# A graph network's degree counts moved into the building stage, and the edge-maximum passes' buffers moved into adjacency tiles

## The chip, the cores and the metric

The kernel runs on one core of a Trainium2 chip as one launch. The metric is the device time of that core in microseconds. It is given as the median of several runs, and one more execution was recorded by the profiler. "Before" and "after" are two versions of one kernel on the same inputs.

## The reference, cut to what matters

The network has 3125 nodes with 96 features and 50000 edges from `src` to `dst`, sorted by `dst`. There are four residual stages, each behind a layer norm and a ReLU. Stage 0 is an attention over the edges with four heads. Stage 1 is two pooling layers, the part that the change touches most. Stage 2 is a sum over weighted edges, stage 3 sixteen steps of propagation.

```python
def _sage_pool_layer(x, src, dst, Wp, bp, Ws, Wn, b, n_nodes):
    m = jax.nn.relu(x @ Wp + bp)
    msgs = m[src]
    agg = jax.ops.segment_max(msgs, dst, num_segments=n_nodes)
    agg = jnp.where(jnp.isfinite(agg), agg, 0.0)
    return x @ Ws + agg @ Wn + b
...
edge_index = jnp.stack([src, dst])
h = jnp.maximum(_layernorm(x, axis=-1), 0.0)
x = x + _L0_gnn_ref(h, L0_gnn_qW, L0_gnn_kW, L0_gnn_vW, src, dst)
h = jnp.maximum(_layernorm(x, axis=-1), 0.0)
x = x + _L1_gnn_ref(h, src, dst, L1_gnn_Wp1, L1_gnn_bp1, L1_gnn_Ws1, L1_gnn_Wn1, L1_gnn_b1, L1_gnn_Wp2, L1_gnn_bp2, L1_gnn_Ws2, L1_gnn_Wn2, L1_gnn_b2)
h = jnp.maximum(_layernorm(x, axis=-1), 0.0)
x = x + _L2_gnn_ref(h, src, dst, edge_weight, L2_gnn_weight_G, L2_gnn_bias_G)
h = jnp.maximum(_layernorm(x, axis=-1), 0.0)
x = x + _L3_gnn_ref(h, edge_index)
```

## The kernel before, in words

**Stages.** Nodes are padded to T = 25 tiles of P = 128 (NP = 3200). The program is a row of stages, each with a block of instructions per engine, and a stage begins when all engines have ended the one before: `front`, `build_adjacency`, `walk_adjacency` (its body is a branch for inputs that overflow the building windows, not taken here), `attention`, `first_layer` (the first dense stage), `max_pass` "max1", `second_layer`, `max_pass` "max2", `third_layer`, `sum_pass` (a branch too), `weighted_layer`, `propagate`. Engines meet through semaphores alone. The order on each engine is the order in which its block writes the instructions.

**`build_adjacency`** makes `adj`, a 3200 x 3200 matrix of fp16 edge counts, 25 tiles `adj[:, k, :]` of 128 partitions by 3200. It works in NGROUP = 200 groups of GROUP = 16 destination nodes. For each group VectorE builds one-hot matrices (ScalarE the first lane matrix, L1260), TensorE multiplies three pairs of them into PSUM (`count`, L1250), and ScalarE copies the result to `adj` (L1269). TensorE's product of a group waits for `kept` of two groups earlier. GpSimd splits the edge weights into two fp16 parts at the start of the stage, SyncE then stores the tables and loads v and the first queries.

**`attention`** works through `adj`, and SyncE saves the last AWAY = 3 tiles of `adj` to DRAM (`away_dram`), since the maximum passes use that place: for the pooled features as two fp16 parts (`pooled_parts`) and, behind them, for one-hot matrices and ids.

**`first_layer`** loads the attention's result, adds it, normalises, and multiplies by the joint weights, tile by tile. On TensorE `turn` (L215) transposes a tile and `multiply` applies the weights. Beside them, `count(n)` (L227) multiplies the columns of one adjacency tile by a column of ones, 25 matmuls a call, to add up every node's degree; eight calls stand ahead of the first tile, one behind each of the first seventeen tiles. ScalarE's first `keep_high`, which writes over the saved tiles, waits until their three are counted. VectorE copies the degrees to `c.deg` at the end of the stage.

**`max_pass`** takes the running maximum over the sorted edges, in NB = 98 blocks of BLK = 512 edges, and beside it builds the weight matrix that `weighted_layer` needs. The blocks m go round one loop, which is written out on each engine; block n = m - 4 is scanned while group m of the weight matrix is laid out. For a block:
- GpSimd gathers 4 x 128 rows of the table in DRAM by index (`indirect_dma_start`, L1736), four gathers a block, into one of RING = 4 row buffers. It waits for `turned`. The eleven blocks in `FAR` are not gathered: TensorE multiplies the pooled parts by one-hot matrices (`add_far`, L1766).
- TensorE transposes the rows (`turn_rows`, L1757), lays out the weight strip (`lay_out`, L1776), spreads the mask (`spread_same`), turns pieces of the finished weight tile (`turn_piece`, L1786) and turns the scanned block back (`turn_back`, L1797).
- VectorE scans (`scan`, L1852: run = max(same x run, column)), builds the next one-hot matrices (L1831, L1833) and keeps the strip's low part.
- ScalarE keeps the mask, the strip's high part (L1919), the turned pieces in `rows_w` (`keep_piece`, L1926) and the turned rows in `out` (`keep_rows`).
- SyncE stores `out` to `rows_dram` (L1968) and, once every four blocks, a finished weight tile from `rows_w` to `weights_dram` (`store_tile`, L1955), two DMAs of 400 KB.

There are two `out` buffers and one `rows_w` buffer. ScalarE's first copy of a piece into `rows_w` for tile i waits for both stores of tile i - 1:

```python
if q == 0 and i >= 1:
    act.wait_ge(rows_stored, 32 * i)
```

TensorE's `turn_piece` waits for ScalarE's copy of the piece before, and `turn_back` stands behind it on TensorE. At the end of a pass (m >= 100) there are no new blocks to lay out, and two pieces are turned at each m. In the first pass alone, TensorE multiplies `upper` (a triangle of ones, made by GpSimd in `first_layer`) and `c.ones` by the degrees, and VectorE's `find_ends` (L1867 on) works out from it the row of every node's last edge, `c.end_row`, which the following dense stages gather by.

In the second pass SyncE loads the three saved tiles back once the last `FAR` block is summed. **`third_layer`** gathers by `c.end_row`, and ends with a copy between halves of the last adjacency tile on SyncE, for which the stage waits.

## Time and profile before

| | us |
|---|---|
| median of 3 runs | 2963.13 |
| lowest and highest | 2960.17, 2963.28 |
| the profiled execution | 2987.34 |
| its span | 2985.5 |
| TensorE busy in the span | 2539.4 (85%) |
| VectorE | 1983.1 (66%) |
| ScalarE | 1225.4 (41%) |
| GpSimd | 1213.3 (41%) |

The mean granted TensorE clock of the profiled execution was 0.914 of full speed. The span is the time from the first to the last recorded instruction. The profiled execution took 24 us more than the median of the runs without a profile, so a sum made from its rows is set against its own time first.

The profile's page calls the engines PE (TensorE; PEld is its weight load, which overlaps the matmuls), DVE (VectorE), ACT (ScalarE), POOL (GpSimd) and SP (SyncE); SPq, POOLq and PEq are their queues. A row names the line of the kernel, the engine, the operation and the tiles, out<-in. A bracket at its end gives the engine's idle time before it and what ended it; "issue" is a wait for nothing that the profile shows, "remote" one for a semaphore without a named setter. The stages lie in the span at about: `front` 0 to 61, `build_adjacency` to 270, `attention` to 678, `first_layer` to 731, the first maximum pass to 1295, `second_layer` to 1376, the second pass to 1934, the third dense stage to 2026, `weighted_layer` to 2170, `propagate` to the end.

### The profile page before, as it was taken

How to read it: one execution, taken by the hardware profiler on the slowest of the kernel's cores; microseconds unless marked ns; L12 is line 12 of the kernel's file. 1: busy time of each engine (PE TensorE's matmuls, PEld its weight loads, DVE VectorE, ACT ScalarE, POOL GpSimd, SP SyncE). 2: the span in 40 equal slices, each digit the busy share in tenths (PEclk: the TensorE clock that was granted, in tenths of full speed). 3: DMA queues.
4: the chain of work that ended last, by engine and by line, in shares of the span. 5: the costliest groups of instructions: out<-in, count | busy, mean ns of one | idle time of the engine just before them, and what ended most of it. 6: DMA issues, size and time to landing. Idle time of an engine off the chain costs nothing. (4 is left out here: it accounts for less than half of the span.)

```text
span 2985.5 us, 67875 instructions
## 1 busy us (share of the span) xinstructions
PE 2539.4 (85%) x26431; PEld 1862.9 (62%) x26431; DVE 1983.1 (66%) x6098; ACT 1225.4 (41%) x2932; POOL 1213.3 (41%) x1428
## 2 busy tenths in 40 slices
PE   6998999997778877747788887557899999999999
PEld 3223777775444444424444444336689999999999
DVE  6998999995788887726889888541234444444444
ACT  5998888884334343423334443330121111111110
POOL 2002999992677776633777777421000000000000
PEclk8999999996999888856999999758999999999999
DMA  6002000004344344442444444517800000000000
GB/s 194 1 1 69 12 12 13 12 11 110 93 110 120 102 105 109 104 85 56 114 102 120 107 105 110 146 44 268 282 5 2 2 2 2 2 2 2 2 2 18
DMA packets 239010, 205.59 MB, mean 69 GB/s; under 512 B 183165, under 2 KB 204442, under 8 KB 238144
## 3 DMA queue, kind: packets, MB, share of 16 engines
q1 hardware_dynamic: 210892, 162.00, 19.5%
q0 software_dynamic: 24256, 37.90, 5.2%
q8 instruction: 214, 3.51, 0.5%
q10 hardware_dynamic: 3540, 1.30, 0.2%
q14 instruction: 108, 0.88, 0.1%
HBM read 103.06 MB, written 100.41 MB: 68 GB/s over the span
## 5 line engine op out<-in xcount | busy, mean ns | idle before, releaser
L1736 POOL DMA_INDIRECT max_row<-table,max_src_rows x696 | 768.6, 1104 | 399.2 <-issue 246.5
L2329 PE MATMUL prop<-g,adj 128*128 128x192 f16 x9216 | 770.6, 246 | 7.1 <-PEq L2000 7.1
L2329 PEld LDWEIGHTS prop<-g,adj 128*128 128x128 f16 x9216 | 759.5, 98 | 14.9 <-issue 12.4
L1630 POOL TENSOR_SCALAR e<-e 128x512 f32<-128x512 f32 (+1 forms) x625 | 365.8, 604 | 244.6 <-ACT e L1618 226.9
L1644 DVE TENSOR_TENSOR e<-e,a_ps 128x1024 f32<-128x1024 f32 (+1 forms) x313 | 371.6, 1194 | 35.1 <-PE a_ps L1556 13.8
L2418 ACT ACTIVATE g<-prop_state 128x96 f16<-128x96 f32 (+1 forms) x375 | 106.0, 283 | 635.1 <-DVE prop_state L2386 635.1
L1618 ACT ACTIVATE e<-s_ps 128x512 f32<-128x512 f32 (+1 forms) x625 | 335.5, 585 | 61.0 <-PE o_ps L1568 38.1
L1776 PE MATMUL max_strip_ps<-max_key_hot,max_lane_w 128*128 128x400 f16 x1200 | 311.4, 369 | 57.3 <-DVE max_lane_w L1833 30.3
L2384 DVE SCALAR_TENSOR_TENSOR part<-prop,coef,prop_base 128x96 f32<-128x96 f32 x384 | 120.5, 314 | 312.8 <-PE prop L2329 226.1
L1926 ACT ACTIVATE max_rows_w<-max_piece 128x896 f16<-128x896 f16 x200 | 168.0, 840 | 378.7 <-remote 164.6
L1833 DVE TENSOR_SCALAR max_lane_w<-iota,max_tables 128x128 f16<-128x128 f16 x1200 | 320.6, 314 | 0.0
L1852 DVE TENSOR_TENSOR_SCAN max_run<-max_same,max_run,max_col 96x512 f32<-96x512 f16 x174 | 221.1, 1271 | 142.6 <-issue 116.0
L1766 PE MATMUL max_far<-adj 128*96 128x512 f16 x1100 | 277.1, 391 | 4.1 <-issue 3.2
L1776 PEld LDWEIGHTS max_strip_ps<-max_key_hot,max_lane_w 128*128 128x128 f16 x1200 | 101.4, 104 | 205.8 <-issue 122.8
L1831 DVE TENSOR_SCALAR max_key_hot<-iota,max_tables 128x400 f16<-128x400 f16 x600 | 188.1, 313 | 35.6 <-remote 17.0
L1250 PE MATMUL count<-key_hot,lane_hot 128*128 128x400 f16 x600 | 195.0, 342 | 19.2 <-ACT lane_hot L1260 7.4
L1766 PEld LDWEIGHTS max_far<-adj 128*96 128x96 f16 x1100 | 139.9, 128 | 109.8 <-issue 17.9
L1568 PE MATMUL o_ps<-e,v_all 128*25 128x128 f32 (+1 forms) x5000 | 197.6, 276 | 5.0 <-DVE e L1644 2.7
L1919 ACT ACTIVATE max_strip<-max_strip_ps 128x400 f16<-128x400 f32 x200 | 101.1, 506 | 244.5 <-PE max_strip_ps L1776 165.9
L1786 PE MATMUL max_piece<-ident,max_strip 128*128 128x128 f16 x1250 | 110.4, 229 | 102.0 <-ACT max_rows_w L1926 76.1
L1546 PE MATMUL s_ps<-q_tile,k_all 96*128 96x128 f16 (+1 forms) x2500 | 190.6, 219 | 4.6 <-DMA k_all<-qk_dram 4.6
L1786 PEld LDWEIGHTS max_piece<-ident,max_strip 128*128 128x128 f16 x1250 | 88.9, 103 | 161.4 <-issue 137.1
(260 smaller groups left out, 3334.2 us busy)
## 6 DMA issues: line engine op xcount, KB each, us to landing
weights<-max_rows_w SPq DMA_DIRECT2D x100, 400.0 KB
rows_dram<-max_out SPq DMA_DIRECT2D x196, 192.0 KB
ws_w<-weights SPq DMA_DIRECT2D x50, 384.0 KB, 5.2
ws_w<-weights SPq DMA_DIRECT2D x50, 288.0 KB, 4.5
max_row<-table,max_src_rows POOLq DMA_INDIRECT x696
ws_w<-weights SPq DMA_DIRECT2D x50, 128.0 KB, 2.7
adj<-ids_dram SPq DMA_DIRECT2D x22, 128.0 KB
q_tile<-qk_dram SPq DMA_DIRECT2D x100, 24.0 KB
```

The source lines that it names most:

```text
L1250: mm = nc.tensor.matmul(count_ps[g % 2][:, 0:KEYS], lane_hot[:, g % RINGS, w, :], key_hot[:, g % RINGS, w, :], start=w == 0, stop=w == WIN ...
L1568: mm = nc.tensor.matmul(o_ps[row % 2][hd * VW:hd * VW + DH + 1, 0:w], v_all[:, t, hd, :], e_tile(u)[:, hd * w:(hd + 1) * w], start=t == 0, ...
L1618: nc.scalar.activation(e_tile(u), s_ps[u % S_RINGS][:, 0:HEADS * width(row)], ACT.Exp).then_inc(exped, 1)
L1630: nc.gpsimd.tensor_scalar(e_tile(u), e_tile(u), math.exp(10.0), math.exp(-10.0), ALU.min, ALU.max).then_inc(clipped, 1)
L1644: nc.vector.tensor_tensor(tile, tile, a.unsqueeze(2).to_broadcast([P, n, HEADS, w]), ALU.mult).then_inc(weighted, 1)
L1736: nc.gpsimd.indirect_dma_start(row[i % RING][:, j, :], None, table_dram, bass.IndirectOffsetOnAxis(ap=src_rows[:, 4 * n + j:4 * n + j + 1] ...
L1766: mm = nc.tensor.matmul(far_ps[0:D, :], parts[:, k, a, :], hot[(T * j + k) % HOTS], start=k == a == 0, stop=k == T - 1 and a == 1)
L1776: mm = nc.tensor.matmul(strip_ps[n % 2][:, 0:KEYS], lane_w[:, w, h, :], key_hot[:, w, :], start=w == 0 and h == 0, stop=w == WIN - 1 and h ...
L1786: tr = nc.tensor.transpose(piece_ps[:, k * P:(k + 1) * P], strip[:, i % 2, first_tile[q] + k, :, :].rearrange("p h d -> p (h d)"), c.ident ...
L1833: one_hot = nc.vector.tensor_scalar(lane_w[:, w, h, :], c.iota16[:, 0:P], at(1), at(2 + h), ALU.is_equal, ALU.mult)
L1852: nc.vector.tensor_tensor_scan(run[n % 2][:, :], same[n % SAME][:, :], cols[0:D, :], run[1 - n % 2][:, BLK - 1:BLK], ALU.mult, ALU.max).th ...
L2329: return nc.tensor.matmul(sums(step, t), adj[:, k, t * P:(t + 1) * P], states[:, k, :], start=start and t % 2 == 0, stop=k == END - 1 and ...
```

## The change

- **Building.** USED_GROUPS = 196 groups are built instead of 200; GpSimd clears the columns of the last four in all tiles. The 625 one-column matmuls that add up the degrees are placed on TensorE between the groups' products, about three ahead of each group, for node tiles whose groups are finished; the last 25 follow the last group. VectorE copies the degrees to `c.deg` at the end of the stage. The branch of `walk_adjacency` counts again, behind its own additions.
- **`first_layer`.** The counting goes out, and with it ScalarE's wait. The two matmuls by `upper` and by `c.ones` and `find_ends` come in, TensorE's ahead of the first transpose, VectorE's ahead of the first group's sums. They go out of the first maximum pass.
- **Five tiles saved.** AWAY is 5 and NEAR_END 3: `attention` saves the last five adjacency tiles. The last three serve as before (`pooled_place`). The two before them (`buffer_place`) hold, in the maximum passes, a second `rows_w` and the third and fourth `out`. The second pass loads the last three back, `third_layer` the two others, behind its copy between the halves, and waits for them at its end.
- **`max_pass`.** `keep_piece` waits for the tile before the previous one, with a semaphore for each buffer; `keep_rows` for the block four earlier. `turn_back` takes every fourth column of the scanned block, so that a partition holds four consecutive rows, and the store to `rows_dram` writes them as one piece.

The diff, cut to its core:

```diff
@@ -48,6 +48,8 @@
...
+USED_GROUPS = -(-N // GROUP)
...
@@ -63,7 +65,8 @@
...
-AWAY = 3
+AWAY, NEAR_END = 5, 3
...
@@ -220,18 +224,9 @@
...
-            def count(n):
...
-                for t in range(T):
-                    mm = nc.tensor.matmul(deg_ps[:, t:t + 1], adj[:, k, t * P:(t + 1) * P], c.ones16[:, :], start=n == t == 0, stop=n == T - 1, skip_group_check=True)
-                if n == AWAY - 1:
-                    mm.then_inc(place_counted, 1)
-                if n == T - 1:
-                    mm.then_inc(counted, 1)
-            for n in range(EARLY):
-                count(n)
+            pe.wait_ge(upper_made, 1)
+            nc.tensor.matmul(ends_ps[:, 0:T], upper[:, :], c.deg[:, :], start=True, stop=True)
+            nc.tensor.matmul(ends_ps[:, T:2 * T], c.ones[:, :], c.deg[:, :], start=True, stop=True).then_inc(ends_summed, 1)
...
@@ -272,9 +265,6 @@
...
-                if g == 0:
-                    act.wait_ge(place_counted, 1)
...
@@ -342,7 +332,25 @@
...
+            def find_ends():
...
+                dve.wait_ge(ends_summed, 1)
...
+                then_wait(nc.vector.tensor_copy(total[:, :], ends_ps[:, T:2 * T]), 1)
+                then_wait(nc.vector.tensor_tensor_scan(before[:, :], c.ones[:, 0:T], total[:, :], 0.0, ALU.mult, ALU.add), 2)
...
+                nc.vector.tensor_copy(c.end_row[:, :], cum[:, :])
...
+            find_ends()
...
@@ -614,7 +620,10 @@
...
+            sp.dma_start(buffer_place(adj), away_dram[:, 0:(AWAY - NEAR_END) * NP]).then_inc(away_loaded, 16)
...
+            sp.wait_ge(away_loaded, 16)
...
@@ -1237,18 +1247,37 @@
...
+            dve.wait_ge(degrees_counted, 1)
+            nc.vector.tensor_copy(c.deg[:, :], deg_ps[:, 0:T])
...
-            for g in range(NGROUP):
+            def count(t, k):
+                return nc.tensor.matmul(deg_ps[:, t:t + 1], adj[:, k, t * P:(t + 1) * P], c.ones16[:, :],
+                                        start=t == k == 0, stop=k == T - 1, skip_group_check=True)
+            for g in range(USED_GROUPS):
...
+                t, i = divmod(g - 1 - TILE_GROUPS, TILE_GROUPS)
+                if t >= 0:
+                    for k in range(T * i // TILE_GROUPS, T * (i + 1) // TILE_GROUPS):
+                        count(t, k)
...
+            t, i = divmod(USED_GROUPS - 1 - TILE_GROUPS, TILE_GROUPS)
+            for k in range(T * i // TILE_GROUPS, T):
+                count(t, k)
+            pe.wait_ge(kept, USED_GROUPS)
+            pe.wait_ge(rest_cleared, 1)
+            for k in range(T):
+                mm = count(T - 1, k)
+            mm.then_inc(degrees_counted, 1)
...
@@ -1447,15 +1479,30 @@
...
-def away(adj):
-    return adj[:, T - AWAY:T, :].rearrange("p k n -> p (k n)")
+                pe.wait_ge(added, STEPS)
...
+                mm.then_inc(recounted, 1)
+def away(adj, first, last):
+    return adj[:, first:last, :].rearrange("p k n -> p (k n)")
+def pooled_place(adj):
+    return away(adj, T - NEAR_END, T)
+def buffer_place(adj):
+    return away(adj, T - AWAY, T - NEAR_END)
...
-    return away(adj)[:, 0:T * 2 * D].rearrange("p (t a d) -> p t a d", t=T, a=2)
+    return pooled_place(adj)[:, 0:T * 2 * D].rearrange("p (t a d) -> p t a d", t=T, a=2)
@@ -1517,7 +1564,7 @@
...
-            sp.dma_start(away_dram, away(adj)).then_inc(away_stored, 16)
+            sp.dma_start(away_dram, away(adj, T - AWAY, T)).then_inc(away_stored, 16)
...
@@ -1674,12 +1720,15 @@
...
-        out = [sb(f"out{i}", [P, 4, D], F32) for i in range(2)]
+        more = buffer_place(adj)
+        out = [sb(f"out{i}", [P, 4, D], F32) for i in range(2)] + [
+            more[:, T * P + 8 * D * i:T * P + 8 * D * (i + 1)].bitcast(F32).rearrange("p (j d) -> p j d", j=4) for i in range(2)]
...
-        written = [sem(f"written{i}") for i in range(2)]
+        written = [sem(f"written{i}") for i in range(OUTS)]
+        rows_stored = [sem(f"rows_stored{i}") for i in range(2)]
...
@@ -1687,18 +1736,15 @@
...
-        rows_w = sb("rows_w", [P, T, P], F16)
+        rows_w = [sb("rows_w", [P, T, P], F16), more[:, 0:T * P].rearrange("p (k n) -> p k n", k=T)]
...
@@ -1791,15 +1837,11 @@
...
-                elif upper is not None:
-                    pe.wait_ge(sums_read, 2)
...
-                    tr = nc.tensor.transpose(back_ps[:, j * D:(j + 1) * D], run[n % 2][:, j * P:(j + 1) * P], c.ident[0:D, 0:D])
+                    tr = nc.tensor.transpose(back_ps[:, j * D:(j + 1) * D], run[n % 2][:, j:BLK:4], c.ident[0:D, 0:D])
...
-            if upper is not None:
-                nc.tensor.matmul(back_ps[:, 0:T], upper[:, :], c.deg[:, :], start=True, stop=True).then_inc(ends_summed, 1)
-                nc.tensor.matmul(back_ps[:, T:2 * T], c.ones[:, :], c.deg[:, :], start=True, stop=True).then_inc(ends_summed, 1)
...
@@ -1920,17 +1939,17 @@
...
-                if q == 0 and i >= 1:
-                    act.wait_ge(rows_stored, 32 * i)
-                nc.scalar.activation(rows_w[:, first_tile[q]:first_tile[q] + PIECES[q], :].rearrange("d k p -> d (k p)"),
+                if q == 0 and i >= 2:
+                    act.wait_ge(rows_stored[i % 2], 32 * (i // 2))
+                nc.scalar.activation(rows_w[i % 2][:, first_tile[q]:first_tile[q] + PIECES[q], :].rearrange("d k p -> d (k p)"),
...
-                if n >= 2:
-                    act.wait_ge(written[n % 2], 16 * (n // 2))
-                nc.scalar.activation(out[n % 2][:, :, :].rearrange("p j d -> p (j d)"), back_ps[:, 0:4 * D], ACT.Copy).then_inc(kept, 1)
+                if n >= OUTS:
+                    act.wait_ge(written[n % OUTS], 16 * (n // OUTS))
+                nc.scalar.activation(out[n % OUTS][:, :, :].rearrange("p j d -> p (j d)"), back_ps[:, 0:4 * D], ACT.Copy).then_inc(kept, 1)
...
@@ -1952,7 +1971,7 @@
...
-                    sp.dma_start(weights_dram[i, h, part, :, :], rows_w[h * HALF:(h + 1) * HALF, :, :].rearrange("d k p -> d (k p)")).then_inc(rows_stored, 16)
+                    sp.dma_start(weights_dram[i, h, part, :, :], rows_w[i % 2][h * HALF:(h + 1) * HALF, :, :].rearrange("d k p -> d (k p)")).then_inc(rows_stored[i % 2], 16)
...
@@ -1965,7 +1984,7 @@
...
-                    sp.dma_start(rows_dram[n * BLK:(n + 1) * BLK, :].rearrange("(j p) d -> p j d", p=P), out[n % 2][:, :, :]).then_inc(written[n % 2], 16)
+                    sp.dma_start(rows_dram[n * BLK:(n + 1) * BLK, :].rearrange("(p j) d -> p j d", p=P), out[n % OUTS][:, :, :]).then_inc(written[n % OUTS], 16)
...
@@ -1976,13 +1995,14 @@
...
-                        sp.dma_start(away(adj), away_dram).then_inc(away_loaded, 16)
+                        sp.dma_start(pooled_place(adj), away_dram[:, (AWAY - NEAR_END) * NP:]).then_inc(away_loaded, 16)
...
-            sp.wait_ge(rows_stored, 32 * T)
...
-                sp.wait_ge(written[b], 16 * len(range(b, NB, 2)))
+                sp.wait_ge(rows_stored[b], 32 * len(range(b, T, 2)))
+            for b in range(OUTS):
+                sp.wait_ge(written[b], 16 * len(range(b, NB, OUTS)))
...
```

## Rows read from the trace of the kernel before

**Rows 1.** Busy time by stage: stretch, us, busy of engines (count), clock, DMA share, GB/s.
```profile
61.00:270.00 209.00, 194.97 (x600) 57.41 (x600) 207.30 (x1000) 205.73 (x600) 2.87 (x3) 0.98 0.04 14
678.00:731.00 53.00, 41.03 (x704) 35.56 (x704) 26.84 (x123) 24.42 (x88) 1.13 (x4) 0.51 0.59 138
731.00:1295.00 564.00, 432.22 (x2615) 252.71 (x2615) 446.85 (x1382) 217.39 (x396) 386.46 (x348) 0.89 0.41 104
1376.00:1934.00 558.00, 429.49 (x2613) 250.81 (x2613) 448.56 (x1374) 214.60 (x396) 382.18 (x348) 0.90 0.42 109
```

**Rows 2.** Timeline of VectorE, scans alone: start us, us, instruction [idle before].
```profile
754.67 1.26 DVE L1852 TENSOR_TENSOR_SCAN max_run<-max_same,max_run,max_col 96x512 f32<-96x512 f16 x1
...
923.01 1.27 DVE L1852 TENSOR_TENSOR_SCAN max_run<-max_same,max_run,max_far 96x512 f32<-96x512 f16 x1
...
959.10 1.27 DVE L1852 TENSOR_TENSOR_SCAN max_run<-max_same,max_run,max_far 96x512 f32<-96x512 f16 x1
...
1283.37 1.28 DVE L1852 TENSOR_TENSOR_SCAN max_run<-max_same,max_run,max_col 96x512 f32<-96x512 f16 x1 [7.91 <-PE max_col L1757]
```

**Rows 3.** The gathers of L1736: count, shortest/median/longest ns, first and last start.
```profile
L1736 POOL DMA_INDIRECT max_row<-table,max_src_rows x696: 938/947/2493, 731.3 to 1907.1; - x174
```

**Rows 4.** Waits of the two passes, 731:1295 and 1376:1934: us, times, longest.
```profile
ACT max_rows_w L1926 <- remote: 68.6, 25, 5.2
...
ACT max_rows_w L1926 <- DMA weights<-max_rows_w: 67.6, 17, 5.8
...
POOL max_row L1736 <- remote: 32.7, 20, 2.9
...
PE max_piece L1786 <- ACT max_rows_w L1926: 28.6, 19, 5.2
...
ACT max_rows_w L1926 <- DMA weights<-max_rows_w: 72.7, 15, 6.0
...
PE max_piece L1786 <- ACT max_rows_w L1926: 47.5, 24, 5.2
...
POOL max_row L1736 <- DMA f_x<-in_x_dram: 31.9, 18, 2.9
```

**Rows 5.** Timelines of SyncE's queue and ScalarE, one weight tile's store and after.
```profile
902.89 1.16 SPq L1955 DMA_DIRECT2D weights<-max_rows_w  x2
...
908.89 0.92 ACT L1926 ACTIVATE max_rows_w<-max_piece 128x896 f16<-128x896 f16 x1 [3.47 <-issue]
...
932.56 0.92 ACT L1926 ACTIVATE max_rows_w<-max_piece 128x896 f16<-128x896 f16 x1 [4.67 <-DMA weights<-max_rows_w]
```

**Rows 6.** Timelines: ScalarE at the end of building, TensorE's first counts.
```profile
267.44 0.50 ACT L1269 ACTIVATE adj<-count 128x400 f16<-128x400 f32 x1 [0.52 <-PE count L1250]
...
269.49 0.50 ACT L1269 ACTIVATE adj<-count 128x400 f16<-128x400 f32 x1 [0.52 <-PE count L1250]
...
679.07 5.45 PE L227 MATMUL l_deg<-ones,adj 128*128 128x1 f16 x200 [2.27 <-PEq L1485]
```

**Rows 7.** Timelines of VectorE and TensorE in `first_layer`, 678 to 731.
```profile
682.59 0.18 DVE L311 TENSOR_SCALAR l_inv<-l_raw 128x20 f32<-128x20 f32 x1 [3.43 <-DMA l_x<-xh_dram]
...
710.54 0.43 PE L215 MATMUL l_turn<-ident,l_h 128*96 128x128 f32 x1
712.11 0.43 PE L215 MATMUL l_turn<-ident,l_h 128*96 128x128 f32 x1
...
720.12 0.42 PE L215 MATMUL l_turn<-ident,l_h 128*96 128x128 f32 x1
720.97 0.42 PE L215 MATMUL l_turn<-ident,l_h 128*96 128x128 f32 x1
```

**Rows 8.** Timelines of ScalarE and TensorE at the first pass's end.
```profile
1280.56 0.92 ACT L1926 ACTIVATE max_rows_w<-max_piece 128x896 f16<-128x896 f16 x1 [3.97 <-DMA weights<-max_rows_w]
...
1281.62 0.80 PE L1786 MATMUL max_piece<-ident,max_strip 128*128 128x128 f16 x6 [5.17 <-ACT max_rows_w L1926]
```

**Rows 9.** Groups of the weight loads by line: busy us, mean ns, idle.
```profile
L1797 PEld LDWEIGHTS max_back<-ident,max_run 96*128 96x128 f32 x784 | 79.0, 152 | 99.4 <-issue 54.7 <-DVE max_run L1852 41.7
```

93 lines of the change are left out of this document (43 added, 50 removed).

## The prediction, made before the changed kernel was run

> **What bounds the kernel now.** I read the busy time by stage first [rows 1]. Building takes 209 us with VectorE busy in 207.3 of them; the first dense stage 53 us with no engine full; the two edge-maximum passes 564 and 558 us, 38% of the time, with VectorE busy 447 us and GpSimd 386. The last stage (`propagate`, 813 us of TensorE) isn't touched.
>
> In a maximum pass the start of VectorE's scan marks a block of 512 edges. The undisturbed pace is 8 blocks from 923.01 to 959.10, 4.51 us each; over all 97 steps from 754.67 to 1283.37 the mean is 5.45 us [rows 2]. So some 0.94 us x 97, about 91 us a pass, is lost to disturbance. VectorE sets the undisturbed pace. GpSimd is the next wall: 348 gathers take 386.46 us, 1.11 us each [rows 1], though the median one takes 0.947 and the shortest 0.938 [rows 3], and with some 0.3 us between two (my estimate, from gather starts about 1.25 us apart where the gathers are short) they need 490 us of the 529.
>
> Which waits make up the loss? ScalarE stands 67.6 and 72.7 us for the previous tile's weights store, and TensorE 28.6 and 47.5 us for ScalarE's copy of a piece [rows 4]. One store: issued at 902.89, the copy that overwrites its buffer starts at 908.89, 6 us later [rows 5]. GpSimd waits 32.7 and 31.9 us for something other than a plain predecessor [rows 4].
>
> **The parts.** *Building.* 196 groups instead of 200. The evacuations at 267.44 and 269.49 are two groups apart [rows 6], 1.025 us a group: 4 x 1.025 = -4.1. The 625 one-column matmuls come in. 200 of them took 5.45 us on TensorE [rows 6], 27 ns each, so three a group cost 0.08 us; TensorE loads weights in only 57 of 209 us while VectorE is full [rows 1], so they hide behind VectorE. Without that cover they would cost 625 x 27 ns = 17 us. Not hidden: the last 25, 0.7 us, and two hand-overs with a 25-column copy, 0.4. The POOL clearing of 64 columns per tile stands ahead of the weight split and of the tables' store on SP; nothing needs these for 200 us, but it shares SBUF with VectorE at the start: +0.5. Sum -2.5; ends 0 and -4.1. The overflow branch is not taken, so its recount runs nothing.
>
> *First dense stage.* Out go the 8 early count groups (they end about when the first group's data arrives, so nothing) and 17 later ones, one beside each tile. With a count group the transposes start at 710.54 and 712.11, 1.57 us apart; without one at 720.12 and 720.97, 0.85 apart [rows 7]. TensorE alone would give 17 x 0.72 = -12.2. But VectorE is busy 26.84 us for 25 tiles [rows 1], 1.07 a tile, and becomes the bound: I take 1.1, so 17 x 0.47 = -8.0. In come the ten end-finding instructions, of about 0.2 us each (a tensor-scalar on a tile of nearly their size took 0.18 [rows 7]), ahead of the first group's sums. VectorE stood idle 3.43 us there until 682.59, waiting for a load [rows 7]; GpSimd's triangle and two cold matmuls have to come before, so I put +1. Term -7; ends -3 (hand-shakes between the root and the scale hold the pace at 1.4) and -12. In the first maximum pass the same ten instructions and two matmuls go out, while GpSimd fills its four row buffers: worth 0, at most -2.
>
> *Second tile buffer, tail.* At the end of a pass nothing runs beside the last tile. There ScalarE waits 3.97 us for the store of tile 24's predecessor, and TensorE 5.17 us for ScalarE [rows 8]; the last scan follows at 1283.37 after 7.91 us of idling [rows 2]. A second buffer removes that wait: -4 in each pass, -8 in all; ends -3 and -10.
>
> *Second tile buffer, and four row buffers, in mid-pass.* The waits to go are TensorE's 28.6 + 47.5 us [rows 4] less the tails' (about 7 each with the two short ones), 62 us. They don't all count. The clean stretch of [rows 2] holds a store wait of 4.67 us before the copy at 932.56 [rows 5], and the pace stayed 4.51. Only a wait in an already late block passes on. What is late next is the gather: GpSimd's own waits, 32.7 + 31.9 us [rows 4], are the most that any freeing of TensorE can give back. Between 0 and -65 I take a third of TensorE's 62, -20, nearer to the clean stretch, where the wait was worth nothing.
>
> *Transposes back.* Each of 784 takes its 128 columns with a step of four fp32, so that a partition's four rows leave as one 1536 B piece, not as four of 384 B. The trace has no stepped load. The nearest row is the load as it is, 152 ns [rows 9]: from nothing up to four times that. Four per block at twice the price would be +0.6 us of TensorE per block. TensorE is recorded busy 432 us for 98 blocks [rows 1], 4.4 us of the 5.45, so 1.0 us a block is free: 0 in the sum. The fewer packets give 0 too: DMA is used to 0.41 [rows 1].
> The Trainium skill ("SBUF — State Buffer", the note on SBUF cachelines) says that reads stay at full bandwidth only while at least two fall into one 16-byte line; a step of four fp32 puts one in each. By it the load would be slower by an amount that the page doesn't give.
>
> *Place of the buffers.* Two more adjacency tiles are saved and reloaded: 1.6 MB more each way. With what [rows 1] moved in the dense stage (138 GB/s at a share of 0.59, so some 234 at full share, read and write) the reload is about 14 us of DMA beside the third dense stage's gathers, and it waits only at the stage's end. +1.5; ends 0 and +5. The longer save during attention ends before the next query load is needed: 0.
>
> **Sum:** -2.5 - 7 - 8 - 20 + 1.5 = -36. The profiled execution took 2987.3 us (span 2985.5), so this would be 2951. The runs shown have their median 24 us below it, at 2963.13; the same difference gives 2927.
>
> **Rivals.**
> *A, the store waits were cover.* Every disturbed block is paced by gathers, and TensorE's freed time goes to waiting for them. For it: the clean stretch, and GpSimd at 490 of 529 us. Against: the tails. Then the mid-pass term is 0: 2963 - 16 = 2947.
> The Trainium skill ("DMA: Bandwidth & Descriptors", SWDGE vs HWDGE vs iDMA) says why gathers lengthen: GpSimd writes their descriptors into SBUF, which VectorE locks it out of in its two-port modes. The mean of 1.11 against a shortest of 0.938 [rows 1, 3] agrees. By that rule a denser VectorE stretches the gathers further, which is this rival.
> *B, the store was the trigger of the late blocks.* Once a block is late, its waits breed others. Then all 65 us of GpSimd's waiting go: -16 - 65, 2882. For it: most of a pass's stores are waited for, 17 and 15 times by name [rows 4]. Against: ScalarE's 68.6 us at the same copy without a named releaser [rows 4], in the first pass, which are not all the store's.
> *C, slower: the stepped load.* If a load costs four times as much, 4 x 0.456 = +1.8 us of TensorE per block. It decides from about +1.0 us a block, that is +0.25 us a load, 0.40 in all; at four times it adds 0.8 x 196 = 157 us, and takes the mid-pass gain: 2963 - 16 + 157 = 3104. At three times, +1.2 a block, it would be 2963 - 16 + 0.2 x 196 = 2986. For it: stepped reads are not in the trace. Against: the load overlaps matmuls.
> *D, it doesn't do what it says:* the counts in the build delay hot matrices and cost as much as they save, and handshakes hold the dense stage at its end of -3; with A's zero in mid-pass and the tails' -8 that is 2963 - 8 - 3 = 2952.
>
> **Chances.** Forecast 0.45, A 0.22, B 0.12, C 0.10, D 0.11. The range: the forecast's own is 2905 to 2942; A and D reach to 2958, and of B I take in the upper half, from 2890. About 0.2% (6 us) is what a measurement of this kernel can tell from no change. Faster: forecast, A, B and D nearly whole, 0.85; same 0.06; slower 0.09 (C for the most part).
>
> **What would show it.** Build: stage shorter by 2 to 3 us, count matmuls between the groups, no new idle time on VectorE. Dense stage: 46 us instead of 53, transposes 1.1 us apart, VectorE without gaps. Passes: the waits for the weights store gone from ScalarE; mean step near 5.3; the last scan's 7.91 us of idling down to 4. GpSimd's waits shrink if the forecast or B holds, and stay with A. C: the `max_back` loads above 400 ns and TensorE without gaps. I am wrong if a clean stretch has steps of more than 4.6 us, or if the passes keep 560 us though the store waits are gone.

## The result, and the profile after

| | before | after |
|---|---|---|
| median | 2961.65 us (6 runs, 2957.24 to 2972.48) | 2943.66 us (6 runs, 2942.72 to 2946.03) |
| profiled execution, its span | 2987.34, 2985.5 us | 2943.83, 2942.1 us |

The ratio is 0.9944, 95% interval 0.993 to 0.9958: 16.6 us off (18.0 between the medians). I had forecast 2927 (-36) within 2890 to 2958. The time lies in the range, but the gain is half of the forecast or a little less, and the time is nearest to rival A (2947).

The trace of before is of a long execution, longer than all six runs; that of after is an ordinary one. So their difference of 43 us overstates the change. This table has the stage lengths (from a stage's first instruction to the next one's; the other columns are runs told of below). In the first pair the two passes differ by 14.4 and 17.0 us; with the dense stage's 10 beside them that is far more than the medians give. 3.8 us more lie ahead of building, in a stage that the change doesn't touch. Times in us.

| stage | before | after | before, chip 8 | changed, chip 6 | changed, chip 12 |
|---|---|---|---|---|---|
| building | 210.4 | 211.3 | 210.3 | 213.0 | 211.4 |
| attention | 406.9 | 408.5 | 407.2 | 408.0 | 408.9 |
| first dense stage | 51.3 | 41.2 | 51.4 | 42.0 | 41.2 |
| first maximum pass | 564.3 | 549.9 | 507.5 | 511.4 | 546.2 |
| second dense stage | 81.6 | 81.0 | 61.7 | 62.8 | 81.0 |
| second maximum pass | 560.2 | 543.2 | 513.3 | 510.0 | 547.1 |
| third dense stage | 94.2 | 94.3 | 77.1 | 77.9 | 94.5 |

Busy time in the kernel after, for the dense stage and the first pass, in the columns of [rows 1]:

```profile
677.70:718.90 41.20, 21.88 (x79) 15.73 (x79) 27.32 (x128) 23.31 (x88) 1.14 (x4) 0.62 0.76 175
718.90:1268.80 549.90, 437.36 (x2613) 266.61 (x2613) 446.46 (x1375) 219.77 (x396) 384.12 (x348) 0.90 0.39 107
```

The dense stage is 10 us shorter, with TensorE busy 21.88 us where it was 41.03. Its start in VectorE's timeline, and two steps in TensorE's:

```profile
679.74 0.18 DVE L341 TENSOR_SCALAR l_has<-deg 128x25 f32<-128x25 f32 x1 [1.90 <-PE l_ends L229]
...
681.95 0.18 DVE L301 TENSOR_SCALAR l_inv<-l_raw 128x20 f32<-128x20 f32 x1 [0.30 <-DMA l_x<-xh_dram]
```

```profile
696.51 0.42 PE L219 MATMUL l_turn<-ident,l_h 128*96 128x128 f32 x1
...
697.36 0.42 PE L219 MATMUL l_turn<-ident,l_h 128*96 128x128 f32 x1
```

The ten end-finding instructions run from 679.74 to 681.65, and VectorE then waits 0.30 us for the load for which it stood 3.43 us in [rows 7]. The first transposes are 0.85 us apart where a count stood between them and made it 1.57; the 25 start from 687.9 to 712.4, before from 688.5 to 724.0. The granted clock was 0.50 of full speed (1.2 GHz) in the whole stage before; after, it was 0.50 until 704.6, with TensorE busy 10.9 of the 11.1 us from 691.9 to 703, and 1.0 (2.4 GHz) from there to 714.9, where steps of 0.44 us stand beside waits of up to 0.81 us for ScalarE.

Building should have been shorter and isn't. Its own instructions are (206.3 us against 208.3). What comes behind them is longer. First ScalarE's timeline before, its first instruction of attention behind the copy at 269.49 of [rows 6]; then the timeline after, from the last instruction of building:

```profile
272.08 1.28 ACT L1611 ACT_TABLE_LOAD   x1 [2.09 <-PEq L1284]
```

```profile
264.04 0.18 DVE L1251 COPY deg<-build_deg 128x25 f32<-128x25 f32 x1 [1.81 <-PE build_deg L1257]
...
269.24 1.28 ACT L1658 ACT_TABLE_LOAD   x1 [6.07 <-PEq L1313]
```

Before, 2.1 us pass from the end at 269.99 to 272.08. After, 5.0 us pass from 264.22 to 269.24, in which no engine is busy. What stands there is the jump over the branch of `walk_adjacency` on TensorE's queue. It has a row when its line is asked for (PEldq is TensorE's queue; count, shortest/median/longest ns, start), first before, then after:

```profile
L1434 PEldq COMPARE_BRANCH  x1: 257/257/257, 271.2 to 271.2; - x1
...
L1466 PEldq COMPARE_BRANCH  x1: 3434/3434/3434, 265.4 to 265.4; - x1
```

The same jump takes 3.43 us instead of 0.26. The other engines' jumps there take 0.05 to 0.07 us in both traces.

The passes' waits, in the columns of [rows 4], for the first and the second pass:

```profile
POOL max_row L1782 <- remote: 33.7, 20, 2.8
...
POOL max_row L1782 <- DMA v_all<-v_dram: 33.7, 16, 3.1
```

ScalarE's waits for the weights store, 67.6 and 72.7 us in [rows 4], have no row any more. TensorE's waits for ScalarE's copy of a piece, 28.6 and 47.5 us there, are 9.0 and 15.6; those for the scanned block rose from 21.8 to 29.0 us in the first pass and from 11.0 to 17.3 in the second. GpSimd's waits (the name behind the arrow is the profile's guess, that DMA was long done), of which I had made the measure of what mid-pass could give back, stand at 33.7 and 33.7 us; before they were 32.7 and 31.9. The end of the first pass:

```profile
1257.58 1.28 DVE L1894 TENSOR_TENSOR_SCAN max_run<-max_same,max_run,max_col 96x512 f32<-96x512 f16 x1 [4.23 <-PE max_col L1803]
```

The last scan's idling fell from 7.91 us [rows 2] to 4.23, as forecast. The stepped weight load, beside [rows 9]:

```profile
L1842 PEld LDWEIGHTS max_back<-ident,max_run 96*128 96x128 f32 x784 | 111.5, 215 | 99.5 <-DVE max_run L1894 57.3 <-issue 36.9
```

215 ns a load against 152 (medians 221 and 141), and the product that follows 286 ns against 246 in the median.

### The profile page after: what moved, and what is told of

The parts are those of the page before. It is cut to its first block and busy times, and to the rows that moved or that the text cites. A ratio compares the mean times of both kernels' runs of the same rounds, so it can differ in the third digit from the quotient of the medians.

```text
span 2942.1 us, 67814 instructions
## 1 busy us (share of the span) xinstructions
PE 2528.8 (86%) x26419; PEld 1892.6 (64%) x26419; DVE 1978.5 (67%) x6078; ACT 1227.1 (42%) x2920; POOL 1216.1 (41%) x1429
## 2 busy tenths in 40 slices
DMA packets 163890, 208.87 MB, mean 71 GB/s; under 512 B 82829, under 2 KB 129194, under 8 KB 162896
## 5 line engine op out<-in xcount | busy, mean ns | idle before, releaser
L1782 POOL DMA_INDIRECT max_row<-table,max_src_rows x696 | 768.5, 1104 | 367.6 <-issue 240.4
L1691 DVE TENSOR_TENSOR e<-e,a_ps 128x1024 f32<-128x1024 f32 (+1 forms) x313 | 371.6, 1194 | 38.6 <-PE a_ps L1603 16.6
L1822 PE MATMUL max_strip_ps<-max_key_hot,max_lane_w 128*128 128x400 f16 x1200 | 296.2, 361 | 72.4 <-issue 36.2
L1812 PE MATMUL max_far<-adj 128*96 128x512 f16 x1100 | 285.9, 398 | 11.8 <-issue 11.6
L1842 PE MATMUL max_back<-ident,max_run 96*128 96x96 f32 x784 | 142.8, 308 | 77.8 <-DVE max_run L1894 46.3
L2409 DVE TENSOR_TENSOR g<-prop_state,g 128x96 f16<-128x96 f32 (+1 forms) x375 | 96.9, 258 | 130.8 <-ACT g L2438 130.8
L1909 DVE TENSOR_SCALAR adj<-adj,node_numbers 128x512 f16<-128x512 f16 x550 | 158.9, 343 | 26.3 <-PE max_far L1812 14.9
```

Source lines behind the costliest of these rows:

```text
L1691: nc.vector.tensor_tensor(tile, tile, a.unsqueeze(2).to_broadcast([P, n, HEADS, w]), ALU.mult).then_inc(weighted, 1)
L1782: nc.gpsimd.indirect_dma_start(row[i % RING][:, j, :], None, table_dram, bass.IndirectOffsetOnAxis(ap=src_rows[:, 4 * n + j:4 * n + j + 1] ...
L1812: mm = nc.tensor.matmul(far_ps[0:D, :], parts[:, k, a, :], hot[(T * j + k) % HOTS], start=k == a == 0, stop=k == T - 1 and a == 1)
L1822: mm = nc.tensor.matmul(strip_ps[n % 2][:, 0:KEYS], lane_w[:, w, h, :], key_hot[:, w, :], start=w == 0 and h == 0, stop=w == WIN - 1 and h ...
```

## The experiments

All times are set beside runs of the kernel before on the same chip. That mattered: the kernel before took 2961 to 2962 us on the first chip and on chips 12 and 13, and 2846 us on chips 8, 6 and 3.

### The passes as before, piece by piece

The passes' changes taken back out of the changed kernel. All three edits together are the first run, each of two alone the next.

```diff
-    SAME, LEAD, HOTS, OUTS = 4, 4, 6, 4
+    SAME, LEAD, HOTS, OUTS = 4, 4, 6, 2
-        rows_w = [sb("rows_w", [P, T, P], F16), more[:, 0:T * P].rearrange("p (k n) -> p k n", k=T)]
+        rows_w = [sb("rows_w", [P, T, P], F16)] * 2
-                if q == 0 and i >= 2:
-                    act.wait_ge(rows_stored[i % 2], 32 * (i // 2))
+                if q == 0 and i >= 1:
+                    act.wait_ge(rows_stored[(i - 1) % 2], 32 * ((i + 1) // 2))
-    run[n % 2][:, j:BLK:4]
+    run[n % 2][:, j * P:(j + 1) * P]
-    rows_dram[n * BLK:(n + 1) * BLK, :].rearrange("(p j) d -> p j d", p=P)
+    rows_dram[n * BLK:(n + 1) * BLK, :].rearrange("(j p) d -> p j d", p=P)
```

> The changed kernel with its maximum passes as before: one tile buffer for the weights, two row buffers out, transposes and store in the old order. What is left of the change is building, the first dense stage and the place of the buffers. Theory 1 (GpSimd's gathers pace the passes, so the waits for the store were mostly cover): the median stands 9 to 12 us below the kernel before, and the changed kernel's further gain of 6 to 9 us is the passes' tails. Theory 2 (the store waits cost time in mid-pass too, and the stepped load gives part of it back): 4 to 9 us below, and nearly all of the passes' gain comes from the buffers. In both, the dense stage takes 41 us as in the changed kernel's trace.

Measured: 2838.91 us, ratio 0.9975 (0.9964 to 0.9985), on chip 8.

The transposes and the store alone:

> The changed kernel, but the transposes back read 128 consecutive columns and the rows are stored as four pieces of 384 B again. The trace of the changed kernel has the load at 221 ns against 141 ns before and the product at 286 against 246. Theory 1 (TensorE has slack, GpSimd paces): no change within 3 us of 2943.7. Theory 2 (TensorE's time counts): 196 blocks x 4 x about 0.1 us is 78 us of TensorE, of which a third passes on: 15 to 25 us faster than the changed kernel. If the packets of 384 B hold up the stores or the gathers, slower by 3 to 10 us.

Measured: 2838.69, 0.9977 (0.9967 to 0.9988). No gain of 15 us, and no loss by the smaller packets.

The tile buffer alone:

> The changed kernel with one tile buffer for the weights: ScalarE waits for the store of the tile before, as in the kernel before; four row buffers and stepped transposes stay. Theory 1: only the two tails lose, 4 us each: +6 to +9 us over 2943.7. Theory 2: mid-pass counts too: +15 to +25 us.

Measured: 2838.28, 0.9976 (0.9966 to 0.9986).

The absolute numbers of the expectations were set for another chip, so only the ratios count, and the three are one: whatever is taken out of the passes, 7 to 8 us below the kernel before are left. The changed kernel itself was not run on this chip. The second trace of before:

> The kernel before once more, for a second trace: its profiled execution took 2987 us where the median is 2962. If the 24 us lie in the maximum passes, their length varies from execution to execution (564 and 558 us in that trace) and single passes can be compared only with this scatter beside them; then the second trace has them shorter, by up to 12 us each. If they lie elsewhere, the passes are 564 and 558 us again.

Measured: 2844.19, 1.0004 (0.999 to 1.0018). Its passes took 507 and 513 us, 50 us less than in the first trace, where 12 us was the scatter that I had allowed for. Busy time and waits in the first pass:

```profile
726.00:1233.00 507.00, 404.35 (x2617) 254.91 (x2617) 447.35 (x1384) 216.75 (x396) 385.62 (x348) 0.93 0.48 116
```

```profile
ACT max_rows_w L1926 <- DMA weights<-max_rows_w: 78.2, 22, 5.2
PE max_col L1757 <- DMA max_row<-table,max_src_rows: 77.8, 43, 3.4
```

ScalarE waits as long for the weights store (78.2 us) as on the first chip. But here TensorE's products wait 77.8 us for the gathered rows, a wait that isn't among the first trace's larger ones, and only 4.1 and 9.8 us for ScalarE's copy, where the first trace had 28.6 and 47.5: on this chip the store waits hardly reach TensorE even with one buffer. That chips differ so much was in neither of my two ideas.

### The changed kernel beside the old passes, on one chip

> The changed kernel, beside the kernel before on one chip. The first two comparisons stand on different chips: there the kernel before took 2962 us, here 2846, and its passes 564 and 560 us against 507 and 513. In the first trace TensorE's signals to VectorE and ScalarE come late in the passes (median 0.6 us, up to 10.7), in the second never. Theory L (the passes' gain is late signals taken off the path): if the kernel before takes about 2960 here too, the changed one is 15 to 25 us faster; if it takes about 2846, 7 us faster, no more than with the passes as before. Theory T (tails): 8 us more than with the passes as before, on either chip.

Measured on chip 6: 2839.83, 0.9971 (0.9957 to 0.9984).

> The maximum passes as before, building and dense stage changed, beside the changed kernel on one chip. Theory L: 7 us faster than the kernel before on either chip; behind the changed kernel by 8 to 15 us where the kernel before takes about 2960, and level with it within 2 us where that takes about 2846. Theory T: behind the changed kernel by 6 to 9 us on either.

Measured: 2837.63, 0.9966 (0.9952 to 0.998). Level, as theory L said for such a chip; theory T's 6 to 9 us are not there.

Of the passes' changes the second tile buffer alone (two `out`, straight transposes):

> The changed kernel with two row buffers and straight transposes: of the passes' changes the second tile buffer alone. Theory L on a chip with late signals: it has most of the passes' gain, within 4 us of the changed kernel, or better by up to 5 us, since the stepped load is out. On a chip without them: level with the changed kernel within 2 us. Theory T: level with the changed kernel within 2 us on either.

Measured: 2832.64, 0.9954 (0.9939 to 0.997): 7 us better than the changed kernel, at the edge of what the intervals can tell (on chip 12, below, the same two are 0.9942 and 0.9943). The changed kernel's waits in the first pass, in the first run of this section:

```profile
PE max_col L1803 <- DMA max_row<-table,max_src_rows: 75.0, 43, 3.8
...
PE max_piece L1832 <- ACT max_rows_w L1945: 2.1, 2, 1.1
```

TensorE's waits for gathers are what they were in the trace of before on chip 8 (75.0 us against 77.8). Its waits for ScalarE's copy are 2.1 us, but they were 4.1 there, so little of TensorE was there to be freed. What ScalarE was freed of, 78.2 us of store waits, went to its waits for TensorE's strips, 182.5 us where they were 130.0.

### A quarter of the gathers left out

Behind the first four blocks, the last of a block's four gathers isn't made, so a quarter of the rows is old.

```diff
-                for j in range(4):
+                for j in range(4 if i < RING else 3):
...
-    pe.wait_ge(gathered[i % RING], 64 * (i // RING + 1))
+    pe.wait_ge(gathered[i % RING], 64 + 48 * (i // RING))
```

> The changed kernel with three gathers of 128 rows a block instead of four, behind the first four blocks; the fourth quarter of a row buffer keeps old rows, so a quarter of the pooled rows is wrong. All else is done as it was. If the gathers pace the passes (GpSimd 490 of 500 us), GpSimd has a quarter less to do and the step falls to VectorE's 4.5 us: 0.45 us x 98 x 2 = 85 us faster where the kernel before takes about 2846. If VectorE or the signals pace them, less than 20 us faster.

Measured: 2729.79, 0.9588 (0.9572 to 0.9603), 110 us below the changed kernel, where 85 was expected. The first 88 steps of a pass took 394.2 and 394.1 us (439.2 and 434.9 with all gathers), 4.48 us each, which is the clean pace of [rows 2]; the rest of the gain is at the passes' ends. The gathers pace the passes on such a chip.

With them off the path, the store waits can be looked at alone. The same kernel with one tile buffer:

> Three gathers a block as in the run before (a quarter of the pooled rows is wrong), and one tile buffer instead of two. There the gathers no longer pace the passes (2729.8 us, median step 4.48). Theory A (the store waits were hidden behind the gathers): they come out where the gathers don't cover them, above all in the two tails: 5 to 12 us slower than 2729.8. If the waits never cost anything but in the tails: 8 us. If mid-pass waits count once the gathers are gone: over 15 us.

Measured on chip 3: 2739.75, 0.9628 (0.9608 to 0.9648), 10 us above the run on chip 6 with two buffers (11 by the ratios). ScalarE's wait in the first pass:

```profile
ACT max_rows_w L1945 <- DMA weights<-max_rows_w: 91.4, 24, 4.9
```

24 waits of together 91.4 us, every store of a tile. And yet the first 88 steps, with 21 of them, took 394.2 us in both passes, as with two buffers: inside a pass they cost nothing even where the gathers are out of the way. ScalarE takes them alone: in these 88 steps TensorE waits for ScalarE's copy 1.5 us in the first pass and not at all in the second. So this run doesn't show what a wait costs that reaches TensorE, as some did in the first trace. The cost is at the end. The last scan, first with one buffer, then with two:

```profile
1166.65 1.27 DVE L1894 TENSOR_TENSOR_SCAN max_run<-max_same,max_run,max_col 96x512 f32<-96x512 f16 x1 [7.81 <-PE max_col L1803]
```

```profile
1164.41 1.27 DVE L1894 TENSOR_TENSOR_SCAN max_run<-max_same,max_run,max_col 96x512 f32<-96x512 f16 x1 [4.02 <-PE max_col L1803]
```

The last step is 9.1 us against 5.3, the idling 7.81 against 4.02 (8.56 against 4.56 in the second pass). That is 3.9 us a pass in the mean by the tail, 7.8 of the 10; the rest is within what two medians of four runs on two chips can tell.

> Three gathers a block, with straight transposes and the rows stored in 384 B pieces. The load goes back from 221 to 141 ns. If VectorE alone sets the step of 4.48 us, level with 2729.8 within 3 us; if TensorE's extra 0.3 us or more a block is on the path once the gathers are off it, 20 to 50 us faster.

Measured: 2728.65, 0.9587 (0.9568 to 0.9607), level; 88 steps took 394.1 and 394.2 us. The stepped load is free in the body of a pass even at VectorE's own pace.

### Chips where the kernel before takes 2961 us

> The changed kernel on one more chip, in the hope of one like the first, where the kernel before takes about 2960 us. Theory L (late signals of TensorE, taken off the path in part): there 15 to 22 us faster than the kernel before, and 7 to 9 us where that takes about 2846.

Measured on chip 12: 2947.51, 0.9943 (0.9921 to 0.9964).

> The maximum passes as before. Theory L: on a chip like the first 5 to 9 us faster than the kernel before and 8 to 15 behind the changed one; where the kernel before takes about 2846, level with the changed kernel.

Measured: 2952.33, 0.9972 (0.9957 to 0.9987). It is 4.8 us behind the changed kernel, and theory L had said 8 to 15.

> The second tile buffer alone of the passes' changes. Theory L: on a chip like the first it has most of the passes' gain, within 4 us of the changed kernel or better; where the kernel before takes about 2846, level with the changed kernel or up to 5 us better.

Measured: 2944.18, 0.9942 (0.9918 to 0.9966). So on such a chip the old passes keep 9.0 of the changed kernel's 13.8 us, and with the second tile buffer alone it is 17.2. The medians give 5 and 8 us for the buffer, each good to some 6. The traces say where: the last step of a pass is 9.2 and 9.2 us before, 9.2 and 9.3 with the old passes; 5.5 and 5.3 after, and 4.4 to 5.8 in the four others of this kind with two buffers and all gathers. In mid-pass they show something else. TensorE's waits for ScalarE's copy in the first pass, with the old passes and then in the changed kernel, both on chip 12:

```profile
PE max_piece L1832 <- ACT max_rows_w L1945: 34.8, 19, 5.2
...
PE max_piece L1832 <- ACT max_rows_w L1945: 28.0, 11, 6.4
PE max_piece L1832 <- ACT adj L1945: 4.0, 1, 4.0
```

(`adj` is the second tile buffer's place.) They are 34.8 us with one buffer and 32.0 with two, in the second pass 36.5 and 37.5. ScalarE's waits for the store are gone, and TensorE's waits for ScalarE are still there. Over both passes the two traces of this kind with one buffer and all gathers have 76.1 and 71.3 us of them, the five with two buffers 22.1 to 69.5. On the chips of 2846 us with all gathers a pass's last step is 6.7 to 10.0 with one buffer (mean 8.4) and 6.5 to 8.8 with two (mean 7.6), so there the tail gives 1 us a pass or so, not 4; with fewer gathers it gives 4 there too, so it is the gathers that keep the end long.

Three gathers a block, with the old passes:

> Three gathers a block (a quarter of the pooled rows is wrong) with the passes otherwise as before: one tile buffer, two row buffers, straight transposes. With one tile buffer and the rest as changed the body of a pass was 394.2 us and the tail 38. If row buffers and transposes are worth nothing here either: 2736 to 2740 us, body 394. If two row buffers are too few once the gathers are off the path, the body is longer by 5 us or more.

Measured: 2798.75, 0.9449 (0.9427 to 0.947), on chip 12, so the absolute forecast doesn't apply; the first 88 steps took 402.4 and 395.8 us. In the second pass two row buffers are enough (395.8). The first pass's 8 us more have signals that come late beside them, so that part stays open.

### The branch that isn't taken

The second count in the overflow branch is 625 matmuls on TensorE that no run here executes. Without them:

```diff
-                pe.wait_ge(added, STEPS)
-                for k in range(T):
-                    for t in range(T):
-                        mm = nc.tensor.matmul(ps[0][:, t:t + 1], adj[:, k, t * P:(t + 1) * P], c.ones16[:, :], ...)
-                mm.then_inc(recounted, 1)
```

> The changed kernel without the second count in the overflow branch, which these inputs don't take: 625 matmuls with their weight loads less on TensorE behind a jump. In the traces of the changed kernel the time from VectorE's last instruction of building to the first of attention is 6.7 us, before it was 2.1, and nothing runs in it. Theory J (the longer jump over the branch costs it, by instructions that have to be fetched behind it): the gap falls to about 2 us and the kernel is 4 to 5 us faster than the changed one, at 0.9955 of the kernel before where that takes about 2846. Rival (the stage's end waits for the degrees' hand-overs or for GpSimd's clearing): the gap stays at 6 to 7 us.

Measured on chip 3: 2831.67, 0.9945 (0.9929 to 0.9962). The place behind building in this run, and the jump:

```profile
270.73 1.28 ACT L1649 ACT_TABLE_LOAD   x1 [3.14 <-PEq L1313]
```

```profile
L1464 PEldq COMPARE_BRANCH  x1: 261/261/261, 269.9 to 269.9; - x1
```

From VectorE's copy, which ends at 268.65, to 270.73 are 2.1 us, where the fifteen traces with the long branch have 5.0 to 6.8 behind the last instruction. TensorE's jump takes 0.26 us, where they have 3.39 to 5.09. Theory J's gap holds, and the rival falls: the hand-overs and GpSimd's clearing are all still there. The whole time is 7 us below the changed kernel's by the ratios (0.9971 on chip 6), where 4 to 5 were expected; the two intervals overlap.

A version that keeps the count, as five reductions and 25 matmuls, with the second tile buffer, two `out` and straight transposes:

```diff
+                for r in range(T // 5):
+                    if r:
+                        dve.wait_ge(recounted, r)
+                    nc.vector.tensor_reduce(key_of[:, 0:5 * P], adj[:, :, 5 * P * r:5 * P * (r + 1)].rearrange("p k n -> p n k"), AX.X, ALU.add).then_inc(added_up, 1)
...
+                for r in range(T // 5):
+                    pe.wait_ge(added_up, r + 1)
+                    for i in range(5):
+                        t = 5 * r + i
+                        mm = nc.tensor.matmul(ps[0][:, t:t + 1], key_of[:, i * P:(i + 1) * P], c.ones[:, 0:1], ...)
+                    mm.then_inc(recounted, 1)
```

> The version that the runs point to: the changed kernel with two row buffers, straight transposes and the second tile buffer, and a branch whose count is 5 reductions on VectorE and 25 matmuls instead of 625. Theory J: the gap behind building is 2 to 3 us, and it is 3 to 5 us faster than the same kernel with the long branch (0.9954 of the kernel before), so about 0.994, some 17 us below the kernel before. Rival: level with 0.9954.

Measured: 2832.69, 0.9946 (0.9929 to 0.9963), 13 us below the kernel before where 17 was expected. From the same passes with the long branch (0.9954) the whole time can't tell it; the stage can: building to attention is 208.4 us (210.3 before, 213.0 changed), and the jump is 0.26 us. Then beside the changed kernel on one chip, 13:

> The changed kernel beside the version with the short branch, on one chip. 7 us faster than the kernel before where that takes about 2846, 14 to 18 us where it takes about 2960.

Measured: 2947.02, 0.9948 (0.9932 to 0.9965).

> Second tile buffer, two row buffers, straight transposes, and the count in the overflow branch by 5 reductions and 25 matmuls. Theory J (the long branch costs 4.4 us behind building): 4 to 7 us faster than the changed kernel on the same chip, whichever it is. If the tile buffer's tails and the branch were both chip-bound, level with it.

Measured: 2938.91, 0.992 (0.9903 to 0.9937): 8 us below the changed kernel and 23 below the kernel before, the fastest of those with all gathers on such a chip. Building is 208.4 us against 211.7, 3.3 of the 8; the rest is within the intervals. These inputs don't take the branch, so its new body has not been run by them.

## Why the prediction was right or wrong

**Building, -2.5: wrong, +1 to +3.** The working of the groups and of the last counts held: the stage's own instructions take 2.0 us less, in the first pair of traces and on chips 8 and 6. The step that failed is the sentence "The overflow branch is not taken, so its recount runs nothing." It runs nothing and still costs 2.9 to 4.7 us, as the run without it shows. The trace of before had a row that warned of it: `sum_pass` has a branch too that isn't taken, and TensorE's jump over it (L2261) took 3386 ns. And attention, 406.9 and 407.2 us before, took 408.0 to 409.4 in 15 of the 18 traces with the longer save, for which I had put 0; that it is the save wasn't tried.

**First dense stage, -7: mis-sized, -10.** Find-ends cost 0.7 us against the 1 assumed (the first group's work starts 4.2 us into the stage, before 3.6). The step that failed is that VectorE "becomes the bound: I take 1.1". Its 1.07 us a tile is busy time over the whole stage, with work before the first and after the last transpose in it; the sixteen steps of 1.57 us became 0.90 in the mean, with TensorE's own pace of 0.85 us as the rule up to 703; that is 10.8 us, of which the last six steps give 0.5 back. The "VectorE without gaps" that should have shown it isn't there: it is busy 27.32 of 41.20 us, and 16.6 of the 20.8 us from the third transpose to the last.

**Tails, -8: right on the kind of chip for which it was made.** The last scan's idling fell by 3.7 and 3.9 us, and 3.8 and 4.0 where the gathers were thinned out. On the other kind it is 1 or so a pass.

**Mid-pass, -20: wrong, 0 shown on one kind of chip.** The step that failed is "The waits to go are TensorE's 28.6 + 47.5 us", with a third of their 62 us passed on to the time. They went only in part with the store waits, from 76.1 and 71.3 us with one buffer to between 22.1 and 69.5 with two. And a store wait that ScalarE takes alone costs nothing: with the gathers thinned out, all 21 in the body of a pass left its 394.2 us as they were. The clean stretch, which I had quoted, was the rule. The same table held a test, GpSimd's waits, and these didn't move. The first pair of traces alone would have confirmed me: TensorE's waits fell from 76.1 to 24.6 us, the first 88 steps by 12 and 18 us, and the mean step came to 5.29 and 5.22 us where I had said 5.3. But the trace of before is of a long execution. The old passes on chip 12 took 468 and 456 us for these steps with 71.3 us of such waits, and after they were 466 and 456 with 24.6 (the trace of the old passes is of the shortest of its ten executions, 7.6 us below their median). For the chips of 2961 us zero is not shown as sharply: 88 steps took 456 to 478 us (mean 469, four passes) with one buffer, and 456 to 471 us (mean 464, ten passes) with two. The medians of the two kernels on chip 12 (2952.33 and 2947.51) leave, beside the tails' 8 us, nothing that can be told from zero.

**Stepped load, 0: right**, at 1.6 times the median of a straight one (221 ns against 141); the rival with four times falls. TensorE's extra 4 x (0.08 + 0.04) = 0.5 us a block went into the 1.0 us that I had counted as free. The 75,000 packets fewer (239010 to 163890 in the page's count) gave nothing either. The Trainium skill's note on SBUF cachelines ("SBUF — State Buffer") was right in its direction: a read that finds one element in each 16-byte line is slower, here by 80 ns in 141.

**Place of the buffers, +1.5: 0 to 1.** The third dense stage took 94.2 and 94.3 us in the first traces, 77.1 and 77.9 on chips 8 and 6 (76.5 to 78.6 in all traces of that kind with the change).

The sum by what was measured, for a chip like the first: building and attention +1 and +1.5, dense stage -10.3, tails -8, the reload 0: -16. The three comparisons of the changed kernel on such chips gave -18.0, -13.8 and -15.0 us in the medians.

**Rival A** said 2947 and got the time and the main point, that mid-pass is worth nothing. That blocks are paced by gathers is shown on the chips of 2846 us, by the run with fewer of them; that the gathers are what made the store waits free is not: with fewer gathers these were free too. Its sum had hidden two errors that cancel: building 3.5 us too good, the dense stage 3 too bad. Its sentence on why gathers lengthen (the Trainium skill, "DMA: Bandwidth & Descriptors", SWDGE vs HWDGE vs iDMA) would have them longer beside a busier VectorE. The traces agree: in the trace of before the 46 gathers that have no instruction of VectorE beside them take 940 to 947 ns, and the 532 for at least 90% of whose time VectorE is busy 1136 in the mean. With a quarter of the gathers left out and VectorE's blocks 4.48 us apart, the mean is 1172 to 1198 ns on chips 6 and 3. The change hardly made VectorE denser (busy 446.9 and 446.5 us in the first pass), and the 696 gathers take 1104 ns in the mean in both.

## What to carry to other kernels

Before a wait is priced, look whether the pace of the loop changes in the iterations that hold it: a wait of 4.67 us in a stretch with an unbroken pace is worth nothing, however often it stands in the table of waits, and its share of the sum should then be the ends of the loops alone, where nothing runs beside it. A wait of a second engine for the first may have another cause than the first one's wait: look whether it goes when that goes. Code behind a jump isn't free because it isn't run: keep a branch that is seldom taken short, on TensorE above all, and ask for the row of the jump itself. Compare ratios on one chip only, and two traces only when both are of ordinary executions.

## What the runs showed of the hardware that was not expected

**Two kinds of chips.** The kernel before took 2846.0 to 2846.8 us on chips 8, 6 and 3, and 2961.3 to 2962.1 on the first, 12 and 13. Each was used at one time alone, so that the kind stays with the chip is not shown. The difference lies in the stages with gathers alone: the passes (507 and 513 us against 564 and 560), the second dense stage (61.7 against 81.6) and the third (77.1 against 94.2). Building, attention and the first dense stage are the same to 0.3 us. In the traces of the slower kind many of TensorE's semaphore signals in a pass arrive late. Of those recorded in the first pass, 423 of 828 come more than 0.6 us after the end of the last instruction that gives them; on chip 8 none of 957. The count is of what the trace kept: of VectorE's signals in that pass 380 of 782 are in the first trace, and 780 on chip 8. One of them, first TensorE's transposes of a block, then VectorE around the scan that waits for them:

```profile
912.24 0.60 PE L1757 MATMUL max_col<-ident,max_row 128*96 128x128 f32 x4
```

```profile
914.79 0.56 DVE L1857 TENSOR_TENSOR max_strip<-max_strip_ps,max_strip 128x400 f16<-128x400 f32 x1
...
919.31 1.27 DVE L1852 TENSOR_TENSOR_SCAN max_run<-max_same,max_run,max_col 96x512 f32<-96x512 f16 x1 [3.96 <-issue]
```

The columns are ready at 912.84. VectorE is free at 915.35, and the scan starts at 919.31, without anything the profile can name in between. With a quarter of the gathers left out on chip 12, 50 of 765 signals were late in the first pass, against 240 of 802 with all of them and the same passes. So they go with the gathers; why one kind of chip does it and the other doesn't, these runs don't show. Of the gap in [rows 2] from the clean 4.51 us to the mean of 5.45, about half is left on chip 8, where the mean is 4.91 and 5.00 us and no signal is late; there it is the gathers. The other half goes with the late signals.

**A skipped branch.** 625 matmuls behind a jump on TensorE cost 2.9 to 4.7 us of empty time, and the jump itself takes 3.39 to 5.09 us in the fifteen traces, against 0.25 to 0.26 in the five whose branch is short. With 25 matmuls and five reductions in the branch it is short too. `sum_pass` pays the same in every trace, 3.39 us before and 3.77 after:

```profile
L2261 PEldq COMPARE_BRANCH  x1: 3386/3386/3386, 2026.8 to 2026.8; - x1
```

No run shortens that branch, so what it would give back is not shown. Fetching of instructions would explain the time, and the DMA view of these 3.4 us in the kernel after fits it: two packets, of 16 and 8 KB, both on queues of the kind "instruction", begin 1.1 us into the jump, and nothing else moves. In the 0.26 us of before none begins.

**A stepped read of weights.** 128 columns of fp32 with a step of four take 221 ns to load against 141 in the median, and the fp32 transpose behind them 286 against 246.

**A gather beside VectorE.** It takes 940 to 947 ns when no instruction of VectorE runs beside it and 1136 in the mean when VectorE is busy nearly all of its time (first trace).
